# Sixteen row buffers for eight, and routed rows scattered over twice as many steps, in an attention and expert-FFN kernel

## What is computed

```python
def reference(x, ctx_1024, ...):
    # q from layernorm(x), k and v from ctx; 16 heads, softmax over 64 keys
    x = x + _L0_xattn_ref(_layernorm(x, axis=-1), ctx_1024, ctx_1024, ...)
    # logits = xf @ Wr.T + br; expert_idx = argmax(logits)
    # h = relu(xf @ W1[e].T + b1[e]); y = h @ W2[e].T + b2[e], the row of expert_idx kept
    x = x + _L0_ffn_ref(_layernorm(x, axis=-1), ...)
    return x
```

## Time and profile before

| | |
|---|---|
| three runs, us | 504.11, 507.33 (median), 508.76 |
| the profiled execution, us | 510.14 |
| its span, first to last instruction, us | 508.3 |
| busy, share of the span | PE 91%, DVE 80%, ACT 62%, POOL 47% |
| mean granted TensorE clock | 0.982 of full speed |
| POOL's scatters (L464) | 64, 63.7 us |
| POOL's outputs (L471) | 71, 70.0 us |

### The profile page before, as it was taken

One profiled execution on the slowest core, in us unless ns is written; L12 is line 12 of the kernel. 1 busy time (PEld: TensorE's weight loads), 2 busy tenths in 40 slices (PEclk: granted clock), 3 DMA queues, 4 the chain that ended last, 5 costly groups with the idle time before them and its releaser, 6 DMA issues.

```text
span 508.3 us, 18979 instructions
## 1 busy us (share of the span) xinstructions
PE 464.8 (91%) x6467; PEld 349.6 (69%) x6468; DVE 408.4 (80%) x1061; ACT 314.4 (62%) x589; POOL 240.2 (47%) x390
## 2 busy tenths in 40 slices
PE   3999968899999999999999999979796989999991
PEld 1665634466666666666666666669686989999991
DVE  4999864678899998999989989878674768777871
ACT  1777755666656666666666666566464667767770
POOL 1558521222232845727447275357575444544552
PEclk9999997999999999999999999999998999999996
DMA  8455300001110211102111039132222322222220
GB/s 276 126 153 149 88 8 16 16 16 22 21 19 17 55 27 35 46 17 50 33 30 50 18 76 373 39 84 64 59 71 65 86 80 69 65 58 72 62 58 0
DMA packets 32745, 33.89 MB, mean 67 GB/s; under 512 B 6675, under 2 KB 26006, under 8 KB 32416
## 3 DMA queue, kind: packets, MB, share of 16 engines
q1 hardware_dynamic: 27840, 24.10, 18.0%
q0 software_dynamic: 4832, 8.80, 5.2%
HBM read 19.14 MB, written 9.99 MB: 57 GB/s over the span
## 4 chain that ended last, share of the span: by engine, by line
PE 58%; DVE 14%; issue 10%; DMA 3%; SPq 2%; ACT 2%; POOL 1%; DVEq 0%; POOLq 0%; ACTq 0%
PE PS L916 10%; PE PS L875 10%; PE PS L1022 10%; PE PS L1035 9%; PE PS L992 5%; PE PS L1001 4%; DVE MX L696 4%; PE PS L946 2%; PE PS L950 2%; PE PS L957 2%; PE PS L1007 1%; PE PS L905 1%; DMA BIG<-rows 1%; ACT PT L527 1%; DVE RD L700 1%
## 5 line engine op out<-in xcount | busy, mean ns | idle before, releaser
L449 POOL TENSOR_TENSOR VP<-BIG,C 128x128 f32<-128x128 f32 x128 | 56.3, 463 | 132.8 <-PE PS L1001 128.4
L696 DVE TENSOR_REDUCE MX<-PS 128x16 f32<-128x1024 f32 x64 | 78.3, 1223 | 28.7 <-PE PS L875 27.4
L916 PEld LDWEIGHTS PS<-C,SB 128*128 128x128 f32 x512 | 54.4, 142 | 67.9 <-ACT SB L544 32.4
L471 POOL DMA_INDIRECT out<-SB,BIG x71 | 70.0, 985 | 64.5 <-DVE SB L847 57.9
L916 PE MATMUL PS<-C,SB 128*128 128x128 f32 x512 | 84.8, 289 | 7.6 <-ACT PT L527 7.2
L544 ACT ACTIVATE SB<-SB 128x1024 f32<-128x1024 f32 x64 | 67.7, 1057 | 23.1 <-DVE SB L704 21.5
L1022 PE MATMUL PS<-BIG,KM 128*128 128x128 f32 x568 | 80.7, 282 | 0.7 <-issue 0.2
L704 DVE TENSOR_TENSOR SB<-PS,MX 128x1024 f32<-128x1024 f32 x64 | 77.4, 1210 | 1.7
L1035 PE MATMUL PS<-KM,SB 128*128 x568 | 76.1, 277 | 0.6 <-ACT SB L561 0.6
L1022 PEld LDWEIGHTS PS<-BIG,KM 128*128 128x128 f32 x568 | 71.6, 193 | 3.8 <-issue 3.1
L464 POOL DMA_INDIRECT rows<-X,DESTI x64 | 63.7, 995 | 22.3 <-issue 15.5
(11 more groups left out here) (123 smaller groups left out, 694.0 us busy)
## 6 DMA issues: line engine op xcount, KB each, us to landing
BIG<-rows SPq DMA_DIRECT2D x71, 66.0 KB
X<-in_x SPq DMA_DIRECT2D x16, 256.0 KB, 3.3
PT<-in_ctxT SPq DMA_DIRECT2D x16, 256.0 KB, 2.9
KM<-BIG SPq DMA_DIRECT2D x240, 16.0 KB
BIG<-in_we SPq DMA_DIRECT2D x1, 2576.0 KB, 10.2
KM<-in_w SPq DMA_DIRECT2D x1, 2048.0 KB, 14.6
out<-SB,BIG POOLq DMA_INDIRECT x71, 2.3
rows<-X,DESTI POOLq DMA_INDIRECT x64
```

What stands on the lines that cost most here:

```text
L449: last = nc.gpsimd.tensor_tensor(dst, v, own, ALU.mult)
L471: nc.gpsimd.indirect_dma_start(out=out, out_offset=bass.IndirectOffsetOnAxis(ap=RT[:, s.r, ID:ID + 1].bitcast(i32), axis=0), in_=YO[:, s.r ...
L696: nc.vector.tensor_reduce(MX[:, n % 2, :], sc, axis=AX.X, op=ALU.max).then_inc(mx_done, 1)
L916: last = nc.tensor.transpose(bank(4)[:, i * P:(i + 1) * P], SB[:, n % 3, hp * P:(hp + 1) * P], ident)
```

## The change

RR becomes 16: sixteen row buffers RT, sixteen output buffers YO (in two thirds of SB in place of one), sixteen semaphores for loads and for outputs, and a body of sixteen blocks wherever `steps` still makes a loop. A batch's eight tiles are scattered one a step, in steps 8j + 23 to 8j + 30, in place of two a step; POOL's part runs four steps longer for it. The integer places DESTI have two buffers, by the batch's parity, and the scatters' semaphores are eight in place of four, so that a batch's places are written once the batch before the last has landed. The first block table is made in steps 56 to 62 in place of 58 to 64.

```diff
-RR = 8
+RR = 16
-        YO = SB[:, 1, :].rearrange("p (r d) -> p r d", r=RR)
+        YO = SB[:, 1:3, :].rearrange("p s (r d) -> p (s r) d", d=D)
-        DESTI = sb("DESTI", P, ST, dt=i32)
+        DESTI = sb("DESTI", P, 2, ST, dt=i32)
-        routed, sent = sems("routed", 4), sem("sent")
+        routed, sent = sems("routed", 8), sem("sent")
...
-            for q in range(4):
-                sp.wait_ge(routed[q], 16 * ST // 4 * (J1 + 1))
-            steps(sp, 0, 3 * RR, RR, load_block(0), peel=RR)
+            for q in range(8):
+                sp.wait_ge(routed[q], 16 * ST // 4 * ((J1 + 2 - q // 4) // 2))
+            for n in range(NB1 - E):
+                load_block(0)(Step(n // RR, n % RR, RR))
             sp.wait_ge(cnt_ready, 1)
             for e in range(E):
-                load_block(0)(Step(3, e, RR))
+                n = NB1 - E + e
+                load_block(0)(Step(n // RR, n % RR, RR))
...
-            for q in range(4):
-                sp.wait_ge(routed[q], 16 * NT // 4)
+            for q in range(8):
+                sp.wait_ge(routed[q], 16 * NT // 8)
...
-                        need(pool, routed[q], 16 * (ST // 4) * j)
+                        need(pool, routed[4 * (j % 2) + q], 16 * (ST // 4) * (j // 2))
                     pool.sem_inc(sent, 1)
-                    nc.gpsimd.tensor_copy(DESTI[:], DEST[:]).then_inc(desti_done, 1)
+                    nc.gpsimd.tensor_copy(DESTI[:, j % 2, :], DEST[:]).then_inc(desti_done, 1)
...
-                    j = s.routing(M_OUT + t // 2)
+                    j = s.routing(M_OUT + t)
...
-            for n in range(STEPS):
+            for n in range(STEPS + ST // 2):
                 masks(Step(n // ST, n % ST, ST))
...
-            steps(pool, STEPS - F0 - 3, NB, RR, home)
+            steps(pool, STEPS + ST // 2 - F0 - 3, NB, RR, home)
...
-                if n == NT - 6:
+                if n == NT - 8:
                     dve.wait_ge(early, 1)
                     blocks_of(FULL, BASE1[:], 0.0)
+                if n == NT - 7:
+                    running_sum(UPTO, FULL)
                 if n == NT - 5:
-                    running_sum(UPTO, FULL)
-                if n == NT - 3:
                     passed(NB1, UPTO)
-                if n == NT - 2:
+                if n == NT - 4:
                     link(nc.vector.tensor_scalar(TABI[:, 0, 1, 0:NB1], ...))
                     link(nc.vector.tensor_scalar(row(GAIN), row(FULL), ...))
-                if n == NT:
+                if n == NT - 2:
                     starts(NB1, GAIN)
```

More of the change, by code:

```diff
@@ L464, in masks @@
                         nc.gpsimd.indirect_dma_start(
-                            out=rows, out_offset=bass.IndirectOffsetOnAxis(ap=DESTI[:, t:t + 1], axis=0),
+                            out=rows, out_offset=bass.IndirectOffsetOnAxis(ap=DESTI[:, j % 2, t:t + 1], axis=0),
                             in_=X[:, j * ST + t, :], in_offset=None,
-                            bounds_check=last_row, oob_is_err=False).then_inc(routed[t % 4], 16)
+                            bounds_check=last_row, oob_is_err=False).then_inc(routed[4 * (j % 2) + t % 4], 16)
             def home(s):
```

## The result

The changed kernel takes **498.78 us** in the median of six runs (497.70 to 501.58), the kernel before 507.54 on the same chip (503.83 to 508.76). The ratio is 0.9845, with a 95% interval of 0.9808 to 0.9882: 1.55% faster, some 8 us. The forecast was 497, between 494 and 502.5.

The account below looks back on a forecast made before the run. PE and VectorE share the pace in attention; PE alone bounds the FFN tail, losing 11.8 us there. Terms -6.69 - 3.08 - 1.6 + 0.2 + 0.3 + 0.7 = -10.2 us give 499.9 profiled, forecast 497, range 494 to 502.5.

Parts of the forecast that it names:

- The stalls: FFN blocks 16 to 20 and 20 to 34: sixteen buffers remove the waits for row loads whole, -6.69 and -3.08 us.
- PE's loops: FFN blocks 40 to 70: writing out PE's loops removes the loss at entry and back-edges, -1.6 us, bounds 0 and 2.01.
- Newton: Attention batches: spread scatters delay the Newton iteration's end on GpSimd to near 183.0, +0.2 us over all five batches.
- The table: Steps 56 to 62: making the first block table sooner puts VectorE work into fuller steps, +0.7 us, bounds 0 and 1.8.
- The end: After the last output: POOL checks more output semaphores, nine of them after that output's, +0.3 us, bounds 0 to 2.4.
- The sum: Whole kernel: all terms together -10.2 us, taking the profiled execution from 510.1 to 499.9 us.
- the last step: Whole kernel: stalls taken as the same in the median run, 2.8 us below the profiled one, so forecast 497.
- The wait: Rival at block 32: late outputs or pad writes keep its wait, gain 7.1, time 500.2 us; chance 0.20.
- The buffers were not the cause: Rival, blocks 16 to 34: load flight or POOL's queue sets the pace, 507 us; chance 0.12 together with late Newton.
- Late Newton: Rival in five batches: a whole scatter lies bare, 6.4 us, time 503; chance 0.12 together with unchanged stalls.
- the port rule: GpSimd's scatters beside busy VectorE: a VectorE instruction can lock descriptor ports, so the DMA waits; would make Newton late.
- Written-out blocks: Rival, PE's FFN blocks: each of 40 once-looped blocks pays 0.67 us, time 524; chance 0.06 with anything like it.

Follow-up runs that it names:

- e1: Kernel before with the ring of row buffers at sixteen and nothing else changed; median 499.1 us, ratio 0.9834.
- e6: Kernel before with sixteen buffers, all FFN loops written out and POOL's last checks in order of issue; median 497.68 us, ratio 0.9810.
- e4: Changed kernel with PE's FFN loops put back at a body of eight; median 500.72 us, ratio 0.9880 to the kernel before.
- e3: Kernel before with only the first block table made two steps sooner; median 506.33 us, ratio 0.9974.
- e5: Kernel before with two destination buffers and eight scatter semaphores, ring of eight, two scatters a step; one run, 16.77 us from block 70 to the end.
- e9: Kernel before with eight scatter semaphores alone; one run, 16.76 us from block 70 to the end.
- e8: Kernel before with the second destination buffer alone; one run, 15.40 us from block 70 to the end.
- e2: Kernel before with one scatter a step, two destination buffers and eight semaphores, but ring of eight and late table; median 506.8 us, ratio 1.0000.

## Why the prediction was right, point by point

**The stalls** (-6.69 and -3.08). The mechanism held throughout, and e1 shows that it is the ring. The working set output 8 at 370.3 and 15 at 387.0, load 32 at 394; they came at 371.42, 388.39 and 395.81, in an execution that reached block 16 1.20 us later than the one of before. Blocks 16 to 20 gave 6.69, 20 to 34 gave 2.73. The missing 0.35 sits in blocks 29 and 32, at 2.06 and 2.05; the one at 32 goes with the loops of the other engines (e6), the one at 29 stays unexplained.

**PE's loops** (-1.6). 58.92 - 57.23 = 1.69 us, near the upper bound as taken; the 0.3 left of 2.01 is block 48 (2.03 us, back to 1.90 in e6) and a longer block 69. The loops' worth as such was under-read: e4 loses another 0.9 us in blocks 16 to 34. In the kernel before those turns lay in the stalled stretch, so the stall terms already held them, and were not all waits for rows as the prediction has it.

**Newton** (+0.2). The timelines of POOL and VectorE at batch 1, answering to the earlier trace rows:

```profile
184.07 0.21 POOL L431 TENSOR_TENSOR X<-YY,Y 128x8 f32<-128x8 f32 x1
...
184.50 0.21 DVE L655 TENSOR_TENSOR PREF<-PS,X 128x64 f32<-128x64 f32 x1
```

This execution runs 1.21 us later than that of before here (261.82 against 260.61 at step 48's maximum). On the clock of before the iteration ends at 184.28 - 1.21 = 183.07, where 183.0 was expected, and VectorE uses it at 183.29 instead of 183.15. Of the 0.72 us of cover 0.22 is left, so nothing is paid: VectorE never stands idle ahead of this use, in any batch, and steps 4 to 56 take 208.23 us for 208.46.

**The table** (+0.7). Measured 0, by the change and by e3. The step that failed is that three of its five parts would lie bare. The stretches from step 56 to 63, the change first and then the kernel before (columns as above):

```profile
293.97:324.05 30.08, 28.93 (x513) 19.59 (x513) 28.91 (x69) 18.74 (x34) 16.76 (x35) 1.00 0.59 200
```

```profile
292.81:323.02 30.21, 29.01 (x513) 19.60 (x513) 28.32 (x67) 18.66 (x34) 16.58 (x35) 1.00 0.58 202
```

VectorE does 0.59 us more in the stretch, and its time without work falls from 30.21 - 28.32 = 1.89 to 1.17. The prediction counted idle time ahead of one instruction, in step 56, and no other; the seven steps together had 1.89 us, three times the 0.59 that came in.

**The end** (+0.3). Measured +1.34. The checks were sized rightly: e1, which has them and the short DRAIN, needs 497.3 - 488.91 = 8.4 us from its last output to the end, 0.3 more than before. The other 1.1 us come from a part that the prediction costed at nothing, the eight semaphores ("they only weaken waits"): that step of it failed, at a place that no view of before lists.

**The sum.** -6.69 - 2.73 - 1.69 + 1.34 and some 0.2 of gain elsewhere make -10.0 against -10.2; so exact a sum is luck: the table came out 0.7 us better and the end 1.0 worse than forecast, and the rest is smaller. Yet the spans differ by 8.5 us and the medians by 8.8, for two reasons. Ahead of step 4 the profiled execution of the change was 1.39 us later, which is no part of it (below). And the last step, that the stalls are the same in a median run as in the profiled one, failed. Blocks 16 to 34 took 43.92 us in the profile that the prediction read, 42.0 to 42.9 in the three others that have a ring of eight and four scatter semaphores, and 40.20 and 39.93 in e5 and e9.

One thing that varied is the flight of block 18's load. Rows of the chain of waits, the kernel before repeated (c1) and then e9:

```profile
385.39 2.77 DMA BIG<-rows
```

```profile
380.51 1.83 DMA BIG<-rows
```

It was 3.92 us in the profile that the prediction read the earlier trace rows; 3.36 and 3.31 in e3 and e8, 2.28 in e5. With it went the granted clock. Blocks 16 to 20 as stretches, c1 and then e9:

```profile
380.85:394.59 13.74, 10.38 (x71) 9.54 (x70) 6.02 (x17) 6.28 (x13) 8.38 (x9) 0.88 0.27 74
```

```profile
375.98:387.30 11.32, 8.83 (x71) 7.91 (x69) 6.11 (x17) 5.90 (x13) 7.59 (x9) 1.00 0.29 78
```

In the kernel before, c1, e3 and e8, where VectorE's longest wait for rows was 2.9 to 4.2 us, PE stood idle and part of the stretch ran at 1.2 GHz (a mean of 0.88 of full speed in all four). In e5 and e9, with longest waits of 2.5 and 2.2 us, all of it ran at 2.4 GHz. That is most of the step from 42 to 40 us: c1 and e5 wait for rows equally long in all (6.4 and 6.5 us), and yet blocks 16 to 34 take 42.01 and 40.20. Some 3.3 us at the lower level, by the mean of 0.88 over 13.74 us, can cost 1.6 (an estimate).

What the profile of before had above c1, e3 and e8 lies elsewhere, at block 32. Its normalise in the kernel before, then in c1:

```profile
418.00 0.34 DVE L830 TENSOR_SCALAR BIG<-BIG 128x128 f32<-128x128 f32 x1 [2.55 <-DMA BIG<-rows]
```

```profile
418.22 0.35 DVE L830 TENSOR_SCALAR BIG<-BIG 128x128 f32<-128x128 f32 x1 [0.95 <-DMA BIG<-rows]
```

So the stall terms, exact for that execution, were 1 to 2 us too large against executions like those three, and -8 to -9 is what was there to gain. e5 and e9, both with eight semaphores and two scatters a step, had the shortest flights of these; whether that is more than chance stays open. The mean clocks of whole executions suggest chance, though the share at the lower level near the end varies too: e3's profile, with the drop in this stretch and none at the start, has 0.991, and four of 32 runs of the kernel before have 0.993, at 503.3 to 504.3 us, so with four semaphores, too, the drop seems to stay away at times.

**The rivals.** The wait did not move in the change: load 32, if it flew 3.92 us again, landed 10.7 us ahead of PE's transpose, where 11 had been worked out. e2, with a ring of eight, shows what is left when outputs alone come sooner: 2.9 us of waits at blocks 30 to 32. "The buffers were not the cause" falls with e1, where 6.69 us go by the ring alone. Late Newton and the port rule show nothing: the 64 scatters take 0.98 to 1.07 us, the longest as before. Written-out blocks cost no more: 103.10 / 54 = 1.909 us each.

## What to carry to other kernels

When a ring of buffers stalls, set its queues forward with a longer ring before touching the order of the work: the length alone brought everything here, and a reordering that only freed buffers sooner shortened the first waits and left the later ones, with no gain that the runs show. See what the ring's length does to loop bodies, since a loop on the engine that sets the pace costs up to 0.6 us a turn here. Read a stall's size, and the granted clock in it, from several executions when a transfer's flight is part of it, and put a bound on edits "at nothing" that touch what runs after the last work.

## What the runs showed of the hardware

The granted clock at the start of the attention steps differs between executions, and so do their times. Stretches from 69 to 87 us (columns as above), the change and then e6:

```profile
69.00:87.00 18.00, 13.20 (x103) 5.74 (x104) 10.93 (x9) 7.79 (x11) 2.35 (x6) 0.72 0.04 9
```

```profile
69.00:87.00 18.00, 12.52 (x168) 5.92 (x168) 13.49 (x12) 10.17 (x15) 3.13 (x8) 1.00 0.06 11
```

In this stretch the pipeline fills and PE waits more than elsewhere (busy 13.20 and 12.52 of 18.00 us, where it was busy 255.5 of 266.0 over the attention steps of the change). Its mean granted clock is 0.72 in three of the twelve profiles, 0.81 in four and 1.00 in five, so part of it ran at 1.2 GHz in seven and all of it at 2.4 GHz in five, and step 4 starts at 85.7 to 86.5, 84.4 to 84.9 and 81.7 to 82.4 us accordingly. That is up to 4.8 us, much of the spread of 503.3 to 511.8 in the runs of the kernel before, and more than the table, the spread and the end together. The prediction has no term for it, since the change doesn't touch it. Why the clock falls in some executions and not in others stays open.
